# Reloads that wait for counted tiles, three partial sums inside the tile loop, and final roots moved from GpSimd to ScalarE and VectorE

## The reference, cut to what matters

```
shared_enc = expert(x, sW1, sb1, sW2, sb2)
weights    = softmax(x @ gW + gb)                 # 15 experts
topv, topi = top_k(weights, 3)
router_enc = sum over the 3 chosen experts of  gate * (gelu(x @ W1[e] + b1[e]) @ W2[e] + b2[e])
y          = shared_enc + router_enc + x
out        = (y - mean(y)) / sqrt(var(y) + 1e-5)
```

## Time and profile before

| what | us |
| --- | --- |
| median of 3 runs | 313.96 (312.1 to 318.12) |
| profiled execution, span from first to last instruction | 310.8 |
| busy: PE, DVE, ACT, POOL | 241.9, 207.7, 191.8, 183.9 |
| mean granted TensorE clock | 0.897 |

### The profile page before, as it was taken

How to read it: one execution, slowest core, us unless ns; L and a number is a source line. 1 busy time by engine, 2 the same in 40 slices (tenths; PEclk the granted TensorE clock), 3 DMA queues, 4 the chain that set the end, 5 groups by cost and what they waited for, 6 DMA issues and landing times.

```text
span 310.8 us, 7030 instructions
## 1 busy us (share of the span) xinstructions
PE 241.9 (78%) x2311; PEld 185.8 (60%) x2311; DVE 207.7 (67%) x572; ACT 191.8 (62%) x423; POOL 183.9 (59%) x169
## 2 busy tenths in 40 slices
PE   1997998868897777796869699999999849995500
PEld 0676767746543334353448277886899849994400
DVE  4478999999999999999557900032555404984550
ACT  2687997729986996666476600055887615884550
POOL 4353344540376737998777777334777775777840
PEclk9999999999999997799799955579999959999755
DMA  7955411105100000792011432212343442635431
GB/s 197 418 180 95 88 19 36 36 3 165 39 2 0 2 3 28 197 391 78 26 43 55 138 98 65 68 46 76 100 116 107 108 157 82 209 105 172 143 102 42
DMA packets 38196, 31.36 MB, mean 101 GB/s; under 512 B 12960, under 2 KB 31408, under 8 KB 37776
## 3 DMA queue, kind: packets, MB, share of 16 engines
q1 hardware_dynamic: 33312, 22.65, 25.2%
q0 software_dynamic: 3520, 7.27, 6.8%
q10 hardware_dynamic: 1328, 0.99, 1.2%
HBM read 19.42 MB, written 11.47 MB: 99 GB/s over the span
## 4 chain that ended last, share of the span: by engine, by line
PE 32%; DVE 30%; issue 11%; POOL 8%; ACT 7%; DMA 7%; SPq 1%; POOLq 0%; DVEq 0%; ACTq 0%
PE psum L916 7%; PE psum L925 6%; PE psum L714 6%; DVE prob_sums L1405 5%; DVE maxes L1399 4%; POOL x_srt L1858 4%; DMA k_heads<-x_srt 3%; POOL y_tok L1920 3%; PE psum L716 2%; PE psum L907 2%; DMA bias_cols<-b_col 2%; ACT q_heads L964 2%; DVE prob_sums L1320 1%; PE psum L524 1%; PE psum L487 1%
## 5 line engine op out<-in xcount | busy, mean ns | idle before, releaser
L1920 POOL DMA_INDIRECT y_tok<-k_heads,y_rows x62 | 63.0, 1016 | 34.7 <-ACT k_heads L1249 19.6
L1858 POOL DMA_INDIRECT x_srt<-v_blocks,slot x48 | 46.8, 975 | 15.4 <-issue 15.4
L1835 POOL TENSOR_TENSOR k_heads<-k_heads,inv_sums 128x1024 f32<-128x1024 f32 x16 | 30.9, 1939 | 24.1 <-DVE inv_sums L1410 24.0
L1241 ACT ACTIVATE k_heads<-psum,k_heads 128x128 f32<-128x128 f32 x94 | 29.4, 363 | 24.0 <-PE psum L916 19.7
L1731 DVE COPY k_heads<-psum 128x128 f32<-128x128 f32 x62 | 17.7, 288 | 38.8 <-PE psum L907 38.4
L916 PE MATMUL psum<-k_heads 128*128 128x128 f32 x188 | 30.3, 286 | 0.4 <-DVE k_heads L1731 0.4
L925 PE MATMUL psum<-k_heads 128*128 128x128 f32 x188 | 30.1, 285 | 0.0
L1823 POOL TENSOR_TENSOR probs<-probs,inv_sums 128x512 f32<-128x512 f32 x16 | 16.7, 1049 | 21.8 <-DVE inv_sums L1325 21.7
L916 PEld LDWEIGHTS psum<-k_heads 128*128 128x128 f32 x188 | 26.0, 200 | 0.8 <-DVE k_heads L1731 0.6
L925 PEld LDWEIGHTS psum<-k_heads 128*128 128x128 f32 x188 | 26.2, 202 | 0.2 <-ACT k_heads L1241 0.2
L907 PE MATMUL psum<-consts,k_heads 128*128 128x128 f32 x62 | 17.7, 289 | 8.8 <-DMA k_heads<-x_srt 8.8
(11 more groups left out here) (176 smaller groups left out, 597.8 us busy)
## 6 DMA issues: line engine op xcount, KB each, us to landing
expert_w<-e_w SPq DMA_DIRECT2D x1, 4369.0 KB, 16.5
k_heads<-x_srt SPq DMA_DIRECT2D x62, 65.0 KB, 1.9
q_heads<-y_tok SPq DMA_DIRECT2D x8, 256.0 KB, 3.7
x_srt<-pad SPq DMA_DIRECT2D x16, 65.0 KB, 3.0
xT<-x_t SPq DMA_DIRECT2D x4, 256.0 KB, 7.0
x_rows<-x_n SPq DMA_DIRECT2D x1, 1024.0 KB, 9.7
ctxT_k<-ctx_k SPq DMA_DIRECT2D x1, 1024.0 KB, 11.9
ctxT_v<-ctx_v SPq DMA_DIRECT2D x1, 1024.0 KB, 13.7
```

The costliest lines, as they stand in the source:

```text
L1241: ins = act.activation(h_tile[:, t % 2, a, :], bank[2 + t % 2][:, P * a:P * a + P], ACT.Gelu, bias=tile_weights(t)[:, EW - 2 + a:EW - 1 + a])
L1835: pool.tensor_tensor(probs2[:, p % 3, :].rearrange("p (t h) -> p t h", t=B), probs2[:, p % 3, :].rearrange("p (t h) -> p t h", t=B), inv_s ...
L1858: pool.indirect_dma_start(out=x_srt, out_offset=bass.IndirectOffsetOnAxis(ap=slot[:, n:n + 1], axis=0), in_=payloads[:, g, k, :], in_offse ...
L1920: pool.indirect_dma_start(out=y_tok, out_offset=bass.IndirectOffsetOnAxis(ap=y_rows[:, t:t + 1].bitcast(mybir.dt.uint32), axis=0), in_=y_t ...
```

## The change

The fixed bounds `DONE_BY` go. VectorE computes after tile 8 not one but four sets of eight counts, one for each quarter. SyncE calls `quarter_landed(c)` after the loads of tiles 33, 45 and 57 and after the last: it reads eight counts of that quarter into registers, waits for them, and issues the reload. The sums of quarters 0, 1 and 2 stand at tiles 40, 50 and 57 and the two following ones, with the statistics at 43, 53 and 60. GpSimd's four powers go. VectorE takes the reciprocal of variance + eps, ScalarE its square root (quarters 0 to 2 in one instruction after the gelu of tile 61, quarter 3 in another), and VectorE refines it with three small operations before -mean * rstd. ScalarE applies the norms of quarters 0 and 1, VectorE those of 2 and 3, by four instructions each.

```diff
-        RELOAD_LAG = 9
-        SUMS_AT = (42, 54)
-        ROOTS_AT = 56
+        RELOAD_AT = (33, 45, 57)
+        SUMS_AT = (40, 50, 57)
...
+            def quarter_landed(c):
+                if c == 0:
+                    sp.wait_ge(s_landed, 1)
+                least = NE if c < NC - 1 else TOPK * T // P
+                landed = [sp.value_load(t_landed[0:1, c, k:k + 1], min_val=16 * (least // NB), max_val=16 * (TABLE // NB))
+                          for k in range(NB)]
+                for k in range(NB):
+                    sp.wait_ge(s_y_scattered[k], landed[k])
+                reload_y(sp, c)
...
-                for c in range(NC - 1):
-                    if t == min(DONE_BY[c] + RELOAD_LAG, NT - 1):
-                        for k in range(NB):
-                            sp.wait_ge(s_y_scattered[k], 16 * -(-(DONE_BY[c] - k) // NB))
-                        reload_y(sp, c)
...
+                if t in RELOAD_AT:
+                    quarter_landed(RELOAD_AT.index(t))
+            quarter_landed(NC - 1)
+            for c in range(NC - 2):
                 sp.wait_ge(s_final, 4 * c + 4)
                 store(sp, c, range(PAIRS))
-            sp.wait_ge(s_final, 4 * NC - 2)
-            sp.wait_ge(s_y_sum, 4 * NC + 1)
+            sp.wait_ge(s_final_v, 4)
+            store(sp, NC - 2, range(PAIRS))
+            sp.wait_ge(s_final_v, 8)
             store(sp, NC - 1, range(PAIRS // 2))
...
+            def root3(c0, c1):
+                act.wait_ge(s_ln3, 3 * c1)
+                act.activation(rstd3[:, 4 * c0:4 * c1], rstd3[:, 4 * c0:4 * c1], ACT.Sqrt).then_inc(s_rstd3, 1)
+
             for i in range(NT + 1):
+                if i == NT:
+                    root3(0, NC - 1)
...
+            act.wait_ge(s_nmean3, 1)
+            for g in range(4 * (NC - 2)):
+                act.activation(acc[:, g, :], acc[:, g, :], ACT.Identity, bias=nmean3[:, g:g + 1],
+                               scale=rstd3[:, g:g + 1]).then_inc(s_final, 1)
+            root3(NC - 1, NC)
+            act.wait_ge(s_final_v, 8)
             store(act, NC - 1, range(PAIRS // 2, PAIRS))
...
+                dve.wait_ge(s_ln3, 3 * c + 2)
+                dve.reciprocal(rstd3[:, 4 * c:4 * c + 4], var_eps3[:, 4 * c:4 * c + 4]).then_inc(s_ln3, 1)
...
+            sum_mean(0, NC - 1, 1)
+            sum_applied(NC - 2, 1)
             for k in range(TOPK):
-                added(NC - 2, k)
...
+                added(NC - 1, k)
             sum_stats(NC - 1)
-            sum_mean(NC - 1)
...
+            sum_mean(NC - 1, NC, 2)
+            sum_applied(NC - 1, 2)
...
-            def rsqrt3(c):
-                pool.wait_ge(s_ln3, 2 * c + 2)
-                pool.tensor_tensor(rstd3[:, 4 * c:4 * c + 4], rstd3[:, 4 * c:4 * c + 4], minus_half[:, :], ALU.pow).then_inc(s_rstd3, 1)
```

More of the change, by code:

```diff
@@ L68 @@
 RUNS = NC * NE
-DONE_BY = tuple((4 * P * TOPK * (c + 1) + NE * (P - 1)) // P for c in range(NC))
 SOON = (NC - 1) * 4 * TOPK
@@ L158, in build @@
         t_data = sb("t_data", [P, 32], I32)
-        used_f = sb("used_f", [1, TABLE + 2])
+        used_f = sb("used_f", [1, TABLE])
+        done_count = sb("done_count", [1, NC])
         t_late = sb("t_late", [1, NB], I32)
-        t_landed = sb("t_landed", [1, NB], I32)
+        t_landed = sb("t_landed", [1, NC, NB], I32)
         logit_sum = sb("logit_sum", [P, NG])
@@ L165, in build @@
         rstd3 = sb("rstd3", [P, NG])
+        var_eps3 = sb("var_eps3", [P, NG])
+        newton3 = sb("newton3", [P, NG])
         nmean3 = sb("nmean3", [P, NG])
@@ L283, in build @@
         s_y_loaded = [sem(f"s_y_loaded{c}") for c in range(NC - 1)]
+        s_final_v = sem("s_final_v")
         s_y_sum = sem("s_y_sum")
@@ L1735, in tiles_landed @@
             def tiles_landed():
[L1737 to L1742, removed]
+                routed(dve.tensor_scalar(done_count[:, :], more_sum[0:1, 1:NC + 1, NE - 1], float(NE), None, ALU.add))
+                for c in range(NC):
+                    routed(dve.tensor_scalar(used_f[:, :], row_consts[0:1, K_T:K_T + TABLE], done_count[:, c:c + 1], 16.0,
+                                             ALU.is_lt, ALU.mult))
+                    with nc.allow_low_precision(reason="whole numbers below 2**24"):
+                        ins = dve.tensor_reduce(t_landed[0:1, c, :], used_f[:, :].rearrange("p (j k) -> p k j", k=NB), AX_X, ALU.add)
+                    if c < NC - 1:
+                        routed(ins)
+                ins.then_inc(s_landed, 1)
             def added(c, k):
@@ L1764, in sum_stats, with sum_mean, sum_applied @@
                 ins.then_inc(s_ln3, 1)
[L1765 to L1771, removed]
+                dve.wait_ge(s_ln3, 3 * c + 1)
+                dve.tensor_scalar(var_eps3[:, 4 * c:4 * c + 4], mean_var3[:, 4 * c:4 * c + 4, 1], EPS, None, ALU.add).then_inc(s_ln3, 1)
+                dve.wait_ge(s_ln3, 3 * c + 2)
+                dve.reciprocal(rstd3[:, 4 * c:4 * c + 4], var_eps3[:, 4 * c:4 * c + 4]).then_inc(s_ln3, 1)
+            def sum_mean(c0, c1, half):
+                gs = slice(4 * c0, 4 * c1)
+                dve.wait_ge(s_rstd3, half)
+                routed(dve.scalar_tensor_tensor(out=newton3[:, gs], in0=var_eps3[:, gs], scalar=-0.5, in1=rstd3[:, gs],
+                                                op0=ALU.mult, op1=ALU.mult))
+                routed(dve.tensor_tensor(newton3[:, gs], newton3[:, gs], rstd3[:, gs], ALU.mult))
+                routed(dve.scalar_tensor_tensor(out=rstd3[:, gs], in0=newton3[:, gs], scalar=1.5, in1=rstd3[:, gs],
+                                                op0=ALU.add, op1=ALU.mult))
+                dve.scalar_tensor_tensor(out=nmean3[:, gs], in0=mean_var3[:, gs, 0], scalar=-1.0,
+                                         in1=rstd3[:, gs], op0=ALU.mult, op1=ALU.mult).then_inc(s_nmean3, 1)
+            def sum_applied(c, half):
+                dve.wait_ge(s_nmean3, half)
+                for g in range(4 * c, 4 * c + 4):
+                    dve.tensor_scalar(acc[:, g, :], acc[:, g, :], rstd3[:, g:g + 1], nmean3[:, g:g + 1],
+                                      ALU.mult, ALU.add).then_inc(s_final_v, 1)
             for c in range(NC - 1):
@@ L1782, in _ @@
                     tiles_landed()
[L1783 to L1786, removed]
+                for c in range(NC - 1):
+                    if t - SUMS_AT[c] in (0, 1, 2):
+                        added(c, t - SUMS_AT[c])
+                    if t == SUMS_AT[c] + 3:
                         sum_stats(c)
@@ L1791, in _ @@
                     expert_of = expert_staged(t + 2, expert_of)
+            sum_mean(0, NC - 1, 1)
+            sum_applied(NC - 2, 1)
             for k in range(TOPK):
-                added(NC - 2, k)
[L1796 to L1802, removed]
-            sum_stats(NC - 1)
-            sum_mean(NC - 1)
[L1805 to L1809, removed]
+                added(NC - 1, k)
+            sum_stats(NC - 1)
+            sum_mean(NC - 1, NC, 2)
+            sum_applied(NC - 1, 2)
         @block.gpsimd
@@ L1922, in _ @@
                     in_=y_tile[:, t % NB, :], in_offset=None).then_inc(s_y_scattered[t % NB], 16)
[L1923 to L1928, removed]
 def layout(inputs):
```

## The result

The changed kernel took 317.81 us (median of 4 runs, 315.5 to 319.54) where the kernel before, run beside it, took 313.03 us. The ratio, for which runs more than 1.5% above the fastest of the same kernel are left out, is 1.0227, with a 95% interval of 1.0166 to 1.0288: slower by 1.7 to 2.9%, 7.1 us by the ratio. The two medians are only 4.8 us apart (1.5%). The forecast was 319 us, +5.1 us, "slower, most likely by less than 2%". The profiled execution has a span of 317.7 us, before 310.8, mean granted clock 0.895 and 0.897.

The account below looks back on a forecast made before the run. Bound: the chain through GpSimd's last power and DRAIN, plus tile loads held behind reloads. Steps summed to an end at 315.9 against 310.8, +5.1 us; on the median 313.96, 319 us. Range 312 to 324.

Parts of the forecast that it names:

- Step 1: Counts after tile 8: six more small VectorE operations, 1.7 us, of which 0.5 shows.
- Step 2: SyncE's counted wait: 5.2 us from tile load to reload, three times more in the loop; 6.5 us of waiting go.
- Steps 3 and 4: First two reloads: tile 34's stall costs 0.5 us in all; tile 46 newly stalls 4.7, low clock adds 2.1.
- rival B: Prefetch hides the second reload: tile loads land in 2 us, stall 2, no clock loss; 314.3 us, chance 0.17.
- Step 5: Third reload and loop's end: landed 6.1 us after issue, tile 61's copy at 298.7, `y_tile` 60 ends at 300.8.
- Step 6: Root on ScalarE: table load 1.28 us, then root, refinement and norms; first store at 305.1, before 294.18.
- rival E: Table switch holds ScalarE for twice its row, another 1.3 us ahead of the root; 320.4 us, chance 0.05.
- Step 7: SyncE's 14 stores without waiting, 0.65 us apart: the last begins at 313.5 and lands at 315.5.
- Step 8: GpSimd without powers reaches the barrier at 313.3, before the stores; gain of 5.2 us at the old end.
- Rival A: All three reloads hold the tile behind them 7.3 us, low clock until loop's end; 4.3 more, 323.5 us, chance 0.25.
- Rival C: Waits go (6.5 us), register reads are hidden, the end follows GpSimd; 306.7 us, chance 0.08.

Follow-up runs that it names:

- r_after2: The changed kernel again, unaltered: 1.0187 times the kernel before in call C, 1.0045 in call B.
- e6_gpsimd: Changed kernel with the four roots back on GpSimd, all behind its last scatter: 1.0396 times the kernel before.
- e1b_const: Changed kernel with constant counts for the first three quarters instead of register reads: 0.9877 times the kernel before in call B, 0.9931 in call A.
- e2_spread: Changed kernel with the same register reads spread over the tile loads: 0.9944 times the kernel before.
- e3_reads: Kernel before with eight register reads ahead of each of its three in-loop reloads, values unused, fixed waits kept: 1.0245 times the kernel before.
- e7_split: Changed kernel with two of quarter 2's four stores moved from SyncE's queue to ScalarE's: 1.0106 times the kernel before.
- e4b_tail: Kernel before in its loop, with the changed kernel's roots, norms and stores: 0.99 times the kernel before in call B, 0.9991 in call A.
- call A: Follow-up runs on one chip beside the kernel before, which took 342.3 us there.
- call B: Follow-up runs on a second chip beside the kernel before, which took 342.2 us there.
- (C): Third call of follow-up runs, on another chip, beside the kernel before, which took 309.6 us there.

## Why the prediction was right, step by step

The time, the sign and the cause came out as forecast; the sizes were off in both directions. The profiled execution rose by 6.9 us, and 2.9 of it is there at tile 33 already (its load at 241.68, before 238.76). Most of that isn't the change: at tile 0 the kernel was 1.0 late and at tile 8 2.5, before the first changed instruction in the loop, and in r_after2 it was 1.1 early at tile 0. The stretch from tile 0 to tile 8 varies between traces: 13.3 us before, 14.8 and 14.7 in the two of the changed kernel, 13.3 in e6_gpsimd, which is the same kernel up to there.

The sum has two parts with opposite signs, and both can be read apart. From the turned copy of tile 8 to the end of `y_tile` 60 it is 75.7 us before, 84.4 in the changed kernel and 83.0 in r_after2: the loop lost 8.7 and 7.4, forecast 9.3. From there to the end of the program it is 19.4 before and 15.0 in both: the tail gave back 4.4, forecast 4.3. From tile 8 on that makes +4.4 and +3.0 where +5.1 was forecast, while the time rose by more than 5.1 by both ratios. That the forecast lies between the two is in part luck.

**Step 1**, counts after tile 8, taken at 0.5: right. From the turning of tile 8 to tile 20 it was 12.9 us before and 13.4 in the changed kernel and in r_after2.

**Step 2**, the price of a counted wait, 5.2: 5.07, 5.49 and 5.09, and 0.2 us of waiting left. Right, and shown apart by three runs: without the reads (e1b_const), with them in idle places (e2_spread), and with them alone (e3_reads).

**Steps 3 and 4**, the stalls. They were 3.48, 2.10 and 3.08 us for the tiles' loads, where I expected about 5 each. I had tile 34 landed 6.5 and tile 46 6.2 after the reload; they were turned 5.3 and 5.4 after it. So the first stall cost nothing against before (tile 37 was 2.1 late, tile 33 2.9), and the second was shorter than 4.7: 2.10 for the tile, but 1.65 more for VectorE, which had the sums and statistics of quarter 0 bunched there. I had put those sums into the stall's shadow; they stood ahead of it. Together they made 3.8, and the clock fell as supposed. That isn't rival B, though it named a stall of 2: tile 46 came 5.4 after the reload and not 2, and the clock did fall. `y_tile` of 49, by which tile 57 may be loaded, came at 284.61 instead of 275.09: 9.5 later, less the 2.5 that came from outside 7.0, predicted 6.9. The sum held with its terms shifted.

**Step 5**: third reload landed 4.7 after issue (6.1 taken), from the reload to tile 61's copy 10.9 (11.4), from there to the end of `y_tile` 60 2.0 (2.1).

**Step 6**: table 1.28, root after 1.30, refinement and -mean * rstd 0.8, norms; from `y_tile` 60 to the first store 4.0 us (4.3). The root begins 1.30 us after the load does, and the load begins at the end of the `y_tile` before it, so rival E fell too. The Trainium skill (ScalarE: Activation LUTs, What ACT_TABLE_LOAD costs) states 2.66 us for a switch with its drain. The trace doesn't agree: the drain has no room there. By that rule the forecast would have been 320.5, 1.021 times its base, which lies inside the measured interval, so only the row decides.

**Step 7**: 14 stores, first to last start 8.6 us (8.45), SyncE never waiting over 0.3. Shown by e7_split.

**Step 8**: GpSimd's DRAIN ends 9.1 after its last work, before the stores. Shown by its end lines in the changed kernel and in e6_gpsimd, and by e4b_tail for the time.

What was off is the verdict's side of 2%: +5.1 forecast, +7.1 by the first ratio and +5.8 by the second (1.0187 of 309.6). The first interval begins just above +5.1, at 5.2, the second holds it (3.1 to 8.5). Rival A's longer shadows are not what made the rest: all three were shorter than its 6.8, and the clock was back before the loop's end (its 319.1 and 4.3 make 323.4, not 323.5). Rival C fell with the reads: they were not hidden.

In parts of the time before: old loop and new tail 0.9991 (call A) and 0.99 (B), new loop without the reads and new tail 0.9877 (B), new loop with them 1.0045 (B) or 1.0187 (C). So the tail is worth 0.1 to 1.0%, the reads in the loop cost 1.7% in call B, and the rest of the loop's change nothing that can be told. Old roots in the new loop, at 1.0396 (C), carry the queue of scatters besides.

## What to carry to other kernels

Before replacing a fixed wait by an exact one, add up what finding the exact number costs on the queue that waits: here 6.5 us of waiting were bought off with 24 register reads of 0.57 us each, 13.7 us on the queue that feeds every tile. Between two waits that the queue has anyway the same reads cost nothing that these runs can tell. And look at how each engine enters the final barrier: an engine whose last small operation ends early may still be the one that ends the program.

## What the runs showed of the hardware that I had not expected

GpSimd's DRAIN at the end lasts 10.1 to 10.7 us in all 14 traces, and it ends 9.1 us behind GpSimd's last work in each, whatever that was: a power (301.5 to 310.6, and 314.1 to 323.2) or a scatter (305.7 to 314.8). VectorE's and ScalarE's take 0.4 to 1.2 us, SyncE's 7 ns.

On the chips of calls A and B the kernel before took 9 to 11% longer, and single instructions have the same durations (a turned copy on VectorE 288 ns on average in the first two traces and in r_after, 289 in e1_const). The time lies between them: in r_after (list of waits; us in total, times, longest) VectorE waits for something that the profile calls remote, where the first two traces have no such wait anywhere. What holds the engines there is open.

```profile
DVE k_heads L1742 <- remote: 9.6, 6, 2.4
```
